# The second norm of 18 tiles by way of memory and VectorE's 32x32 blocks instead of TensorE transposes

## What is computed

```python
x = x + xattn(layernorm(x), ctx, ctx, W_proj, b_proj)     # |key - query| <= 64
# ffn of y = layernorm(x); the scan runs over the batches, c starts as in_c
ft = sigmoid(xt @ wf.T + c @ uf.T + bf)
it = sigmoid(xt @ wi.T + c @ ui.T + bi)
gt = tanh(xt @ wc.T + c @ uc.T + bc)
c = ft * c + it * gt
h = tanh(y @ wo.T + c_final @ uo.T + bo)
x = x + h
```

## Time and profile before

| | |
|---|---|
| median of 3 runs | 956.67 us (954.79 to 958.66) |
| profiled execution | 956.46 us, its span 954.6 us |
| TensorE busy | 97% of the span |
| VectorE, ScalarE, GpSimd busy | 70%, 50%, 21% |
| granted TensorE clock | 0.997 of full speed |
| packets of the main DMA queue | 98776, 37.8% of 16 engines' time |

### The profile page before, as it was taken

One profiled execution on the slowest core, in us unless ns is written; L12 is line 12 of the kernel. 1 busy time (PEld: TensorE's weight loads), 2 busy tenths in 40 slices (PEclk: granted clock), 3 DMA queues, 4 the chain that ended last, 5 costly groups with the idle time before them and its releaser, 6 DMA issues.

```text
span 954.6 us, 21946 instructions
## 1 busy us (share of the span) xinstructions
PE 924.4 (97%) x7888; PEld 723.1 (76%) x7888; DVE 664.2 (70%) x2263; ACT 476.3 (50%) x1430; POOL 202.9 (21%) x228
## 2 busy tenths in 40 slices
PE   5889999899999999999999999999999999999998
PEld 3545666688888888888888888888888888878887
DVE  6888898878779877897789867986798522142222
ACT  5887667655445544655545546555555412131222
POOL 4475322211111111111111111111111000003444
PEclk9999999999999999999999999999999999999999
DMA  9554422233333334333433234333322040049862
GB/s 287 166 163 149 117 88 75 67 104 93 95 107 116 108 104 111 106 107 106 115 109 100 83 104 117 95 85 84 96 85 68 24 154 1 1 161 389 294 246 100
DMA packets 99604, 114.15 MB, mean 120 GB/s; under 512 B 9384, under 2 KB 66728, under 8 KB 97960
## 3 DMA queue, kind: packets, MB, share of 16 engines
q1 hardware_dynamic: 98776, 112.47, 37.8%
q10 hardware_dynamic: 720, 0.27, 0.2%
HBM read 82.98 MB, written 29.74 MB: 118 GB/s over the span
## 4 chain that ended last, share of the span: by engine, by line
PE 88%; DVE 4%; ACT 3%; issue 3%; POOL 1%; DMA 1%; SPq 0%; DVEq 0%; ACTq 0%; POOLq 0%
PE ps_g L633 18%; PE ps_g L635 17%; PE ps_g L634 17%; PE ps_a L670 5%; PE ps_a L692 5%; PE ps_m L633 4%; PE ps_v L713 3%; PE ps_m L635 3%; PE ps_m L634 3%; PE ps_m L745 2%; PE ps_v L718 2%; ACT probs L841 2%; PE ps_a L633 2%; PE ps_a L635 2%; PE ps_a L634 2%
## 5 line engine op out<-in xcount | busy, mean ns | idle before, releaser
L841 ACT ACTIVATE probs<-probs,rowmin 128x192 f32<-128x192 f32 (+1 forms) x512 | 239.5, 470 | 87.7 <-DVE rowmin L948 87.6
L948 DVE CUSTOM_DVE_ANT_0 probs<-ps_a,mask 128x192 f32<-128x192 f32 (+1 forms) x512 | 167.3, 386 | 50.5 <-PE ps_a L670 49.7
L883 ACT ACTIVATE gate<-ps_g,bias 128x512 f32<-128x512 f32 x84 | 57.7, 687 | 183.5 <-PE ps_g L635 183.1
L633 PE MATMUL ps_g<-state_hi,gate_w 128*128 128x512 f32 x336 | 133.5, 397 | 0.0
L635 PE MATMUL ps_g<-state_hi,gate_w 128*128 128x512 f32 x336 | 131.1, 390 | 0.0
L634 PE MATMUL ps_g<-state_lo,gate_w 128*128 128x512 f32 x336 | 130.8, 389 | 0.0
L983 DVE STREAM_TRANSPOSE keys<-probs 32x128 f32<-32x128 f32 x420 | 126.0, 300 | 5.4 <-issue 0.2
L841 ACT ACTIVATION_READ_ACCUMULATOR probs<-probs,rowmin 128x1 f32 x512 | 96.4, 188 | 0.0
L612 POOL TENSOR_TENSOR attn_lo<-recip,attn_hi 128x512 fp32r<-128x512 f32 x23 | 29.8, 1294 | 283.4 <-ACT attn_hi L854 283.4
L846 ACT ACTIVATE probs_t<-ps_a 128x512 f32<-128x512 f32 x108 | 59.4, 595 | 51.9 <-PE ps_a L692 51.9
L633 PE MATMUL ps_g<-x2t_even,gate_w 128*128 128x512 f32 x192 | 80.0, 417 | 0.0
(11 more groups left out here) (203 smaller groups left out, 1723.2 us busy)
## 6 DMA issues: line engine op xcount, KB each, us to landing
values<-ctx_rows SPq DMA_DIRECT2D x34, 256.0 KB, 4.4
xr<-x SPq DMA_DIRECT2D x32, 256.0 KB, 3.9
keys<-ctx_t SPq DMA_DIRECT2D x16, 512.0 KB, 4.9
x_dram<-xr SPq DMA_DIRECT2D x32, 256.0 KB, 5.4
gate_w<-x2t_dram SPq DMA_DIRECT2D x8, 1024.0 KB, 10.0
keys<-ctx_t SPq DMA_DIRECT2D x16, 384.0 KB, 3.5
x2t_dram<-x2t_even SPq DMA_DIRECT2D x12, 512.0 KB, 3.9
x2t_dram<-x2t_odd SPq DMA_DIRECT2D x12, 512.0 KB, 3.9
```

The lines of the kernel that those rows point to most:

```text
L633: pe.matmul(ps, lhs[0], rhs[0], start=start, stop=False)
L841: act.activation(row, row, ACT.Exp, bias=rowmin[:, i % 2, h:h + 1], scale=-1.0, accum_out=rowsum[:, i // G % 2, i % G, h:h + 1]).then_inc( ...
L883: act.activation(gate[:, min(gt, 1), :], ps_g[i % 2][:, :], ACT.Tanh, bias=(first_bias if b == 0 else bias)[:, gt, m:m + 1], scale=1.0 if ...
L948: dve.tensor_tensor_reduce(probs[:, i % 2, h, 0:SEEN[t]], ps_a[h][:, score_at[i]:score_at[i] + SEEN[t]], mask[:, MASK0[t]:MASK0[t] + SEEN[ ...
```

## The change

From tile 8 on, every tile whose `t` is 0, 1 or 2 is in `MOVED`: 8, 9, 10, 12, 13, 14 and so on to 28, 29, 30, 18 tiles. For these, TensorE no longer transposes `x2`. SP writes the normed tile to `x2_dram` after `ln2b`, waits until it has landed, and reads it back with four DMAs, one for each 32 rows, so that the block of rows a and columns m lies on partitions 32m to 32m + 31 of the low half of `x2t`. VectorE then turns the 32x32 blocks with one transpose into `tile_row`, ScalarE rounds that for the high half, VectorE subtracts for the low one. In the list, `turn2` and `turn2_lo` of these tiles stand behind the last portion of cells of the `s == 2` step, no longer behind the first. The norm rows wait for `x2_lo`, since `tile_row` is free only then.

```diff
--- before.py
+++ after.py
@@ -19,7 +19,7 @@
 
 
 def bass_xattn_ffn(nc, x, x_t, ctx_rows, ctx_t, w_proj, b_proj, w_gates, u_gates, biases, w_out, u_out, b_out, in_c,
-                   out, x1_dram, x2t_dram, recip_dram):
+                   out, x1_dram, x2_dram, x2t_dram, recip_dram):
     B, T, D = x.shape
     TT = T // P
     G = D // P
@@ -71,6 +71,20 @@
     TURNED_X = SENT + 2
     XR = 4
     PAIR = 2
+
+
+
+    MOVED = [j for j in range(SENT - 1, TILES) if j % TT < TT - 1]
+
+    def moved(n):
+        return sum(j < n for j in MOVED)
+
+    def moves_landed(n):
+        return DMA * (P // BLK) * moved(n)
+
+    def by_tensor(n):
+        return n - moved(n)
+
     chunks = [(gt, u, k) for gt in range(NG) for u in (1, 0) for k in range(0, G, PAIR)]
     NCH = len(chunks)
 
@@ -155,11 +169,11 @@
             cells(2)
             if s == 0 and i + 1 < TURNED_X:
                 tile_steps("query", i + 1)
-            if s == 2:
+            if s == 2 and i - 1 not in MOVED:
                 tile_steps("turn2", i - 1)
             gates(2)
             steps.extend(("score", m) for m in ahead[:1])
-            if s == 2:
+            if s == 2 and i - 1 not in MOVED:
                 tile_steps("turn2_lo", i - 1)
             steps.extend(("score", m) for m in ahead[1:])
             if s == 0:
@@ -194,6 +208,9 @@
             if s == 0:
                 tile_steps("ln2b", i - 1)
             else:
+                if i - 1 in MOVED:
+                    tile_steps("turn2", i - 1)
+                    tile_steps("turn2_lo", i - 1)
                 if i + 2 < TILES:
                     steps.append(("norm_rows", i))
                 tile_steps("bias", i + 2)
@@ -389,7 +406,7 @@
         x1_out = [sem(f"x1_out{r}") for r in range(XR)]
         x2t_out = [sem("x2t_out0"), sem("x2t_out1")]
         recip_sent = sem("recip_sent"); recip_in = sem("recip_in")
-        xt_in = sem("xt_in"); norm_in = sem("norm_in")
+        xt_in = sem("xt_in"); norm_in = sem("norm_in"); x2_sent = sem("x2_sent"); x2_moved = sem("x2_moved")
         raw_in = sem("raw_in"); bo_in = sem("bo_in")
         x2t_in = {b: sem(f"x2t_in{b}") for b in range(B - 2)}
         x1_in = [sem(f"x1_in{r}") for r in range(X1_RING)]
@@ -403,7 +420,7 @@
         centred = sem("centred")
         masked = sem("masked"); inverted = sem("inverted"); inv_turned = sem("inv_turned"); padded = sem("padded"); banks_zero = sem("banks_zero"); turned_b = sem("turned_b"); cleared = sem("cleared")
         attn_t = sem("attn_t"); x1_done = sem("x1_done")
-        stat2 = sem("stat2"); aggr2 = sem("aggr2"); var2 = sem("var2"); x2_done = sem("x2_done"); x2_lo = sem("x2_lo")
+        stat2 = sem("stat2"); aggr2 = sem("aggr2"); var2 = sem("var2"); x2_done = sem("x2_done"); x2_lo = sem("x2_lo"); x2_blocks = sem("x2_blocks")
         in_gate = sem("in_gate"); kept = sem("kept"); cell = sem("cell"); c_lo = sem("c_lo")
         bias_half = sem("bias_half"); c0_zero = sem("c0_zero"); c0_lo = sem("c0_lo")
         column_turned = sem("column_turned"); column_sum = sem("column_sum"); biased = sem("biased")
@@ -498,6 +515,17 @@
                 if kind == "ln2b":
                     sp.wait_ge(x1_done, i + 1)
                     sp.dma_start(x1_rows[i], xr[:, i % XR, :]).then_inc(x1_out[i % XR], DMA)
+                    if i in MOVED:
+                        sp.wait_ge(x2_done, i + 1)
+                        if t == 0:
+                            sp.wait_ge(gate_sum, UNITS * (b - 1))
+                            sp.wait_ge(x2t_out[b % 2], DMA * TT * (b // 2))
+                        sp.dma_start(x2_dram[i], x2[:, :]).then_inc(x2_sent, DMA)
+                        sp.wait_ge(x2_sent, DMA * moved(i + 1))
+                        for a in range(P // BLK):
+                            blocks = x2_dram[i, BLK * a:BLK * (a + 1), :].rearrange("r (k m c) -> m r k c", m=P // BLK, c=BLK)
+                            home = x2t[b % 2][:, 1, :, t * P + BLK * a:t * P + BLK * (a + 1)]
+                            sp.dma_start(home.bitcast(F32), blocks).then_inc(x2_moved, DMA)
                 if kind == "send":
                     sent = i - SENT
                     sp.wait_ge(inv_turned, sent + 1)
@@ -510,7 +538,9 @@
                     sp.dma_start(recip_row, rows.unsqueeze(1).to_broadcast([HPG, HEAD, D])).then_inc(recip_in, DMA)
                 if kind == "norm_rows":
                     sp.wait_ge(recip_sent, DMA * (i - SENT + 1))
-                    sp.wait_ge(x2_turned, i)
+                    sp.wait_ge(x2_turned, by_tensor(i))
+                    if i - 1 in MOVED:
+                        sp.wait_ge(x2_lo, i)
                     sp.wait_ge(q_ready, i + 2)
                     for a, row in enumerate((MEAN + 2 * (i % 2), RSTD + i % 2)):
                         sp.dma_start(norm_rows[:, a, :], recip_dram[i, row, :].partition_broadcast(P))                          .then_inc(norm_in, DMA)
@@ -753,7 +783,7 @@
                             mm = product(ps_m[:, :], (attn_hi[:, k, :], attn_lo[:, k, :]),
                                          (proj_w[:, 0, k, :], proj_w[:, 1, k, :]), k == 0, k == G - 1)
                     mm.then_inc(projected, 1)
-                if kind == "turn2":
+                if kind == "turn2" and i not in MOVED:
                     pe.wait_ge(x2_done, i + 1)
                     need(pe, q_ready, min(i + 3, TURNED_X))
                     need(pe, column_turned, len([n for n in row_at if n < G * (i + 1) + 2]))
@@ -859,7 +889,12 @@
                         act.activation(proj_w[:, 0, k, :], wp[:, k, :], ACT.Copy).then_inc(wp_hi, 1)
                 if kind == "turn2":
                     b, t = i // TT, i % TT
-                    act.wait_ge(x2_turned, i + 1)
+                    if i in MOVED:
+                        act.wait_ge(x2_blocks, moved(i + 1))
+                        act.activation(x2t[b % 2][:, 0, :, t * P:(t + 1) * P], x2[:, :].rearrange("p (k q) -> p k q", k=G),
+                                       ACT.Copy).then_inc(x2_hi, 1)
+                        continue
+                    act.wait_ge(x2_turned, by_tensor(i + 1))
                     if t == 0 and b >= 2:
                         act.wait_ge(gate_sum, UNITS * (b - 1))
                         act.wait_ge(x2t_out[b % 2], DMA * TT * (b // 2))
@@ -924,7 +959,7 @@
                     dve.wait_ge(rstd1, i + 1)
                     need(dve, q_turned, i)
                     if i > SENT:
-                        dve.wait_ge(x2_turned, i - 2)
+                        dve.wait_ge(x2_turned, by_tensor(i - 2))
                     if i - 2 < WHOLE:
                         need(dve, projected, i - 1)
                     elif i <= SENT + 1:
@@ -1010,15 +1045,24 @@
                     r = i % 2
                     dve.wait_ge(rstd2, i + 1)
                     dve.wait_ge(q_turned, min(i + 3, TURNED_X))
-                    need(dve, x2_turned, i)
+                    need(dve, x2_turned, by_tensor(i))
                     if i + 2 >= TURNED_X:
                         dve.wait_ge(q_ready, min(i + 3, TILES))
                     dve.tensor_scalar(x2[:, :], xr[:, i % XR, :], mv2[:, r, 0:1], rs2[:, r:r + 1],
                                       ALU.subtract, ALU.mult).then_inc(x2_done, 1)
+                if kind == "turn2" and i in MOVED:
+                    b, t = i // TT, i % TT
+                    dve.wait_ge(x2_moved, moves_landed(i + 1))
+                    dve.transpose(x2[:, :].rearrange("p (k q) -> p k q", k=G),
+                                  x2t[b % 2][:, 1, :, t * P:(t + 1) * P].bitcast(F32)).then_inc(x2_blocks, 1)
                 if kind == ("turn2_lo" if isinstance(i, int) and i + 1 >= SENT else "turn2"):
                     b, t = i // TT, i % TT
                     cols = slice(t * P, (t + 1) * P)
                     dve.wait_ge(x2_hi, i + 1)
+                    if i in MOVED:
+                        dve.tensor_tensor(x2t[b % 2][:, 1, :, cols], x2[:, :].rearrange("p (k q) -> p k q", k=G),
+                                          x2t[b % 2][:, 0, :, cols].bitcast(F32), ALU.subtract).then_inc(x2_lo, 1)
+                        continue
                     dve.tensor_tensor(x2t[b % 2][:, 1, :, cols], ps_m[:, :].rearrange("p (k q) -> p k q", k=G),
                                       x2t[b % 2][:, 0, :, cols].bitcast(F32), ALU.subtract).then_inc(x2_lo, 1)
                 if kind == "halve_c0":
...
```

More of the change, by code:

```diff
@@ L1142 @@
     B, T, D = arrays["x"].shape
+    x2_dram = nc.dram_tensor("x2_dram", (B * T // P, P, D), F32, kind="Internal").ap()
     recip_dram = nc.dram_tensor("recip_dram", (B * T // P, HEAD, P), F32, kind="Internal").ap()
@@ L1146 @@
                    [d["w_c"], d["w_i"], d["w_f"]], [d["u_c"], d["u_i"], d["u_f"]],
-                   [d["b_c"], d["b_i"], d["b_f"]], d["w_out"], d["u_out"], d["b_out"], d["in_c"], out, x1_dram, x2t_dram,
-                   recip_dram)
```

(2 more changed lines are left out.)

## The result

The changed kernel takes 1006.55 us (median of 6 runs, 1003.76 to 1009.19) against 956.04 us for the kernel before beside it (6 runs, 954.79 to 958.66): the ratio is 1.0526, 95% interval 1.0501 to 1.0551. The profiled execution took 1007.96 us, its span 1006.1. The forecast was 1022 us, slower, within 968 to 1095.

A forecast was written before the change was run, and what follows sets the result against it. TensorE, busy 97% of the span and 88% of the chain, was taken as the bound. Its net lateness in moved tiles, 6 x 5.9 + 6 x 2.7 + 5 x 2.8 = 65.6 us, added to 956.5 gave 1022 us, range 968 to 1095.

The forecast's parts named there:

- the signs that were named: Reads landing 8 us or more after issue, VectorE idle some 4 us, TensorE waiting 2 to 6 us per moved tile.
- Step 1: Write to `x2_dram`, queued behind the broadcast read and x1 write: lands 6.05 us after the x1 write's issue.
- Step 2: The four reads back from `x2_dram`: 2048 packets shared by four engines, 512 packets each.
- Steps 3 and 4: Read-back: 14 ns per packet gives 7.2 us; with 1.15 us before first data and 0.35 after last, 8.7 us.
- tile 30: Last moved tile: no score or value follows it, so its lateness costs nothing.
- Step 5: VectorE and ScalarE work from the blocks to the last side blocks: 4.7 us, or 5.65 for t = 0.
- the deadlines: Starts of TensorE's second value products, which need the side blocks: missed by 5.9, 2.7 and 2.8 us (t = 0, 1, 2).
- The tie with SP's queue: Query load behind `x2_lo` and norm rows: 2.7 us late beside 2.8 on the other path, covered by TensorE's lateness.
- What it removes: Four TensorE transposes in each of 18 tiles, 0.44 to 0.53 us per tile: 7.9 to 9.5 us, all on the path.
- A: Rival, chance 0.10: 16 engines serve the reads, blocks back some 3.7 us after the write lands; 956.5 us.
- B: Rival, chance 0.08: the round trip fits into the slack, nothing waits and the whole gain is kept; about 948 us.
- C: Rival, chance 0.06: a 128 B packet read costs what a 512 B one does, 33.1 ns; 1187 us.

The follow-up runs named there:

- e12: e9 without the wait of TensorE's projection for the subtraction of the moved tile before it: 950.72 us, ratio 0.9941.
- e2: e1 with the broadcast read of the reciprocals issued as four DMAs, so that it too uses 16 engines: 957.57 us, ratio 1.0011.
- e5: Changed kernel with e1's write in four pieces and one read per tile, in runs of 512 B over 16 engines: 956.4 us, ratio 1.0001.
- e1: Changed kernel with the tile stored as four 128x128 blocks, so that its four reads go over all 16 engines: 962.69 us, ratio 1.0064.
- e9: Changed kernel, same round trip, with a moved tile's turning, rounding and subtraction put into the next tile's first step: 994.87 us, ratio 1.0401.
- e8: Changed kernel with 20 idle TensorE matmuls ahead of the scores in each step of a moved tile with t = 0: 1000.31 us, ratio 1.0472.
- e4: Changed kernel with only the tiles of t = 1 and 2 moved, 12 instead of 18: 973.05 us, ratio 1.0173.
- e7: e5 with the reciprocals' broadcast read on all 16 engines as in e2: 956.81 us, ratio 1.0005.
- e13: e12 with the transfers of e7, one read per tile and the reciprocals' read on all 16 engines: 950.28 us, ratio 0.9936.
- e6: Changed kernel with the second norm's turning, its subtraction and the norm rows behind the step's last side blocks: 1006.96 us, ratio 1.0534.

## Why the prediction was right, and which sizes were off

**Direction and mechanism: right.** The loss comes from VectorE waiting for the blocks, with the rounding, the blends, the side blocks and SP's loads queued behind it. Moved away from that place, the same round trip costs nothing (e12). Of the signs that were named, VectorE's idle time (18 times, 3.5 us) and TensorE's two waits came out, 2.1 us a moved tile for both together. Reads that land 8 us or more after issue, at a quarter of the DMA view, did not: 6.9 us, at a third.

**Step 1, the write's landing: right in cause, a little short.** 6.05 us from the x1 write's issue were forecast; tile 16 shows 6.2, tile 17 shows 6.7 (451.30 to 458.02), and 14 of the 18 moved tiles lie between 6.4 and 7.3. e2 shows the cause, the four-engine read, by removing it.

**Step 2, four engines: right.** Each read has four packets that signal, where the one read of e5 has 16, and e1 is what 16 engines bring. The rule that the prediction set beside this step, of the Trainium skill's page "DMA: Bandwidth & Descriptors", section "Why a DMA increments its semaphore by 16 and not by 1", agrees with both: four signals and 54 GB/s with 4 outermost groups, landing in 2.3 us with 128.

**Steps 3 and 4, the packet's price: mis-sized.** 14 ns were taken between bounds of 12.0 and 33.1. All three come from the share of the engines' time, so they are how long a packet lasts; the sum used them as the distance from one packet to the next. The new reads (DMA view, window 430 to 434 us) and the 132 packets of the earlier trace rows (the GB/s of their window) show the two apart:

```profile
q1 hardware_dynamic: 1613, 0.20, 32.7%
```
```profile
GB/s 0 0 0 0 0 0 0 0 0 0 0 0 0 0 0 0 0 20 32 51 59 51 59 47 59 51 59 16 0 0 0 0 0 0 0 0 0 0 0 0
```

A new packet lasts 13.0 ns (32.7% of 16 engines over 4 us, by 1613), as the 12.9 of the 132 said. But 1613 in 4 us on four engines is one every 9.9 ns, 9.5 where the rate is flat. The 132 came at mostly 51 to 59 GB/s, one every 9 to 10 ns, so the distance could have been read before the run. The second leg took 6.9 us in most tiles, not 8.7: the data 4.85 instead of 7.2, the fixed parts 2.0 instead of 1.5. The figure of the Trainium skill that the prediction named beside this step (page "DMA: Bandwidth & Descriptors", section "Bandwidth", 10.5 ns) is nearer to the 9.5 of the trace, which is still below it.

**What the sum makes of it.** With both legs as measured, 13.6 us from the x1 write's issue to the transpose over the 18 tiles instead of 14.75, my estimate of the sum is 1022 - 17 x 1.2 = 1002 us, and 1006.55 was measured. So terms that the prediction had at nothing (the clock, tile 30) made up for some of what it had too high; that the forecast is only 15 us off is in part luck.

**Step 5 and the deadlines: right for t = 0.** Tile 16's side blocks were ready 5.2 us behind the blocks (5.65 forecast), and its value products start 17.69 us after `ln2b` (423.01 to 440.70), not 14.02 as before (407.19 to 421.21): late by 3.7 where 5.9 was forecast. Of the difference the second leg gives 1.8 and this step 0.4. From there to the next `ln2b` the trace adds another 2.1 us (11.39 against 9.28), with the projection at half clock.

**Tile 30, put at nothing: wrong.** The prediction let it cost nothing, as no score or value product follows. But the projection follows, and it waits for the subtraction of the moved tile:

```profile
820.93 0.71 PE L663 MATMUL ps_m<-proj_w,attn_hi 128*128 128x512 f32 x1 [2.37 <-DVE x2t_odd L1063]
```

The period behind tile 30 is 3.8 us longer than before, with a stretch at half clock from 821 on. It is the wait that e9 ran into in every moved tile.

**What the prediction left out: the clock.** It had TensorE's waits as their own cost alone. e8 puts the clock at some 6 us of the 50 (by the intervals, 1 to 10). Taking away only the idleness at t = 0 (e8), or the move of those tiles (e4), ended the three stretches at t = 2 too; why is open.

**The tie with SP's queue at t = 1 and 2: near in size, wrong in who wins.** The value products of tile 17 are late by 1.3 us (469.36 - 452.09 against 16.01), those of tile 18 not at all (15.98 against 16.69). What makes the next `ln2b` late there is VectorE's wait for the queries:

```profile
471.11 0.58 SPq L549 DMA_DIRECT2D queries<-x_t  x1
...
478.46 0.69 DVE L973 TENSOR_TENSOR queries<-queries,tile_row 128x512 f32<-128x512 f32 x1 [2.55 <-DMA queries<-x_t]
```

The tiles with t = 1 come out at 2.5 us on average against 2.7, the five with t = 2 that the forecast counted at 1.7 against 2.8. The load shown is issued 19.0 us after `ln2b`, not 17.4, and VectorE has it after 7.4, not 5.4. That this alone sets these tiles is read from the trace; no run took it apart.

**Give-back, not forecast:** the tile that is not moved made up 4.1 us over five batches.

**What it removes: over-sized.** 7.9 to 9.5 us were put down for the transposes. Where the chain is TensorE's again (e12), the kernel gained 5.8 us, 0.32 per tile. That the distance between two starts holds some time that the next group needs anyway is one reading; no run shows it.

**Rivals.** A (16 engines, 956.5 us): e1 made it, at 962.7. From the first read's issue to the transpose it took 5.3 us for one tile of e1 (439.65 to 444.98), where 3.7 had been put down: the four issues took 0.7 us each, not 0.55. e5 and e7, whose one read lands in 2.8 us, come out where A did, at 956.4 and 956.8, and for its reason: t = 0 late by 0.9 us in A, by 1.1 in e5. B needed the round trip to fit into the slack and the whole gain to be kept: at that place it fits in 17 of 18 tiles of e5, but the gain is not kept; one step later most of it is (e12 and e13, 950.7 and 950.3, against B's 948). The rule of the Trainium skill that the prediction set beside B (page "DMA: Bandwidth & Descriptors", section "Anatomy of one DMA") is fitted there to transfers issued from GpSimd, and all of these are issued from SP. For an x1 write my estimate by it is 2.6 us; the writes land in 2.2 us in e2 and in 5.6 behind the four-engine read. C needed 33.1 ns from packet to packet and is excluded by the 9.5.

## What to carry to other kernels

Hand a slow round trip's result to a consumer that stands a whole step later in every engine's order, and look through all engines for waits that only the old data path needed; then its length and its engine count hardly matter. Shortening the round trip in its old place only came back to even. Where one item is freed from a shared wait, look at what else stands behind the same wait, and at what the new order puts off (e6). And when a rate is read from a profile, keep apart how long a packet lasts and how far apart two of them start.

## What the runs showed of the hardware that was not expected

- A strided read of 128 B runs on four engines streams at 54 GB/s. A packet lasts 13.0 ns, but an engine takes one every 9.5 ns.
- SP spends 1.06 us on each issue of such a read (4.24 for four), 0.7 on the same 64 KB in the form that 16 engines share (2.84 for four in e1), and 0.38 on the one read of 256 KB of e5.
- After TensorE had stood for 2.4 us in tile 16's step, its granted clock was at its lower level for some 7 us. It does not follow each such wait: eight of the 18 moved tiles show it, and what tells them from the others is open.
- Half clock costs less than its arithmetic here: 31 us of it taken away gave some 6 us, at most 10 by the intervals (e8), and half of 31 is 15.5.
